# A gather-bound graph network layer: sets of groups, destinations broadcast by DMA, and one tile of 25 built from on-chip columns

## What is computed

```python
h = maximum(layernorm(x), 0)                       # 12500 x 128
m = relu(concat([h[src], h[dst], ea]) @ w1 + b1) @ w2 + b2     # one row per edge
agg = segment_sum(m, dst)                          # 12500 x 128
gi, gh = agg @ w_ih + b_ih, h @ w_hh + b_hh        # GRU gates
r, z = sigmoid(i_r + h_r), sigmoid(i_z + h_z)
n = tanh(i_n + r * h_n)
out = x + (1 - z) * n + z * h
```

## Time and profile before

| what | value |
|---|---|
| median of 3 runs | 4001.74 us (4001.74 to 4002.7) |
| the profiled execution: own time | 4009.54 us |
| its span, first to last instruction | 4007.8 us |
| mean granted TensorE clock | 0.87 |
| first and last gather begin | 76.1 us and 3988.8 us into the span |
| busy share PE, PE weight load, DVE, ACT, POOL | 75%, 67%, 43%, 32%, 75% |
| DMA | 288 MB, mean 72 GB/s |

### The profile page before, as it was taken

The page is one execution under the profiler, slowest core; times in us unless marked ns, Lnnn a source line. Parts: engine busy times, 40 slices in busy tenths (PEclk is TensorE's granted clock), DMA queues, the critical chain, the costliest instruction groups (busy, mean ns, idle before and its releaser), DMA issues.

```text
span 4007.8 us, 76313 instructions
## 1 busy us (share of the span) xinstructions
PE 2996.9 (75%) x20157; PEld 2691.1 (67%) x20157; DVE 1716.2 (43%) x6014; ACT 1281.7 (32%) x3575; POOL 2991.4 (75%) x3163
## 2 busy tenths in 40 slices
PE   5777777777777777777777777777777777777777
PEld 4667666667666666666666667666666666766666
DVE  6444444444444444444444444444444444444443
ACT  5333333333333323333333333333333333333332
POOL 4777777777777777777777777777777777777776
PEclk8888889888888888888888888888888888888887
DMA  6222222222222222222222222222222222222222
GB/s 187 68 69 69 69 69 69 69 69 70 69 69 69 70 70 69 69 69 70 69 69 69 69 69 70 69 69 69 70 69 69 69 69 69 69 69 69 69 69 56
DMA packets 275619, 287.99 MB, mean 72 GB/s; under 512 B 153847, under 2 KB 204696, under 8 KB 275475
## 3 DMA queue, kind: packets, MB, share of 16 engines
q0 software_dynamic: 100000, 205.00, 20.4%
q1 hardware_dynamic: 147282, 69.63, 6.1%
q10 hardware_dynamic: 28318, 13.14, 1.2%
HBM read 274.60 MB, written 12.83 MB: 72 GB/s over the span
## 4 chain that ended last, share of the span: by engine, by line
POOL 71%; issue 26%; DMA 1%; POOLq 1%; DVE 1%; PE 1%; ACT 0%; SPq 0%; DVEq 0%; ACTq 0%
POOL rows L423 71%; POOLq L227 1%; DMA p_rows<-low 1%; POOLq L238 0%; DMA acc<-in_x_dram 0%; DVE stats L700 0%; PE ps L1032 0%; PE ps L1005 0%; DVE mv L706 0%; DVE dst_int L779 0%; DMA onehot<-base_f_dram 0%; DVE low L725 0%; PE ps L1093 0%; PE ps L1094 0%; ACT low L505 0%
## 5 line engine op out<-in xcount | busy, mean ns | idle before, releaser
L423 POOL DMA_INDIRECT rows<-p_rows,idx x3125 | 2960.9, 947 | 964.4 <-issue 952.3
L574 ACT ACTIVATE lhs<-ps 96x640 f32<-96x640 f32 x625 | 437.6, 700 | 2590.5 <-PE ps L1008 2585.4
L1032 PE MATMUL ps<-onehot,rows 128*128 128x95 f32 x6250 | 915.1, 298 | 427.0 <-ACT rows L580 425.9
L1032 PEld LDWEIGHTS ps<-onehot,rows 128*128 128x128 f32 x6250 | 830.6, 210 | 520.9 <-ACT rows L580 290.4
L800 DVE TENSOR_TENSOR rows<-rows,ps 128x640 f32<-128x640 f32 x625 | 512.7, 820 | 1341.3 <-DMA rows<-p_rows,idx 1335.2
L1019 PE MATMUL ps<-rhs,lhs 128*128 128x128 f32 x6250 | 983.8, 315 | 68.9 <-DVE rows L800 68.4
L1019 PEld LDWEIGHTS ps<-rhs,lhs 128*128 128x128 f32 x6250 | 919.0, 229 | 97.2 <-issue 89.9
L1005 PE MATMUL ps<-ident,onehot 128*96 128x128 f32 x3125 | 547.6, 315 | 475.0 <-DVE onehot L790 473.8
L1005 PEld LDWEIGHTS ps<-ident,onehot 128*96 128x96 f32 x3125 | 385.6, 145 | 567.7 <-DVE onehot L790 560.2
L790 DVE TENSOR_SCALAR onehot<-iota_w,dst_int 128x95 f32<-128x95 f32 x3125 | 736.1, 298 | 51.1 <-issue 51.0
L580 ACT ACTIVATE rows<-rows 128x640 f32<-128x640 f32 x625 | 460.0, 736 | 84.6 <-DVE rows L800 82.1
(11 more groups left out here) (94 smaller groups left out, 1307.9 us busy)
## 6 DMA issues: line engine op xcount, KB each, us to landing
rows<-p_rows,idx POOLq DMA_INDIRECT x3125
lhs<-in_ea_t_dram SPq DMA_DIRECT2D x625, 80.0 KB
idx<-in_src_cols_dram SPq DMA_DIRECT2D x625, 2.5 KB
p_rows<-low SPq DMA_DIRECT2D x14, 448.0 KB, 3.6
x_fin<-in_x_dram ACTq DMA_DIRECT2D x123, 50.0 KB
out_dram<-out_fin ACTq DMA_DIRECT2D x123, 50.0 KB
acc<-in_x_dram SPq DMA_DIRECT2D x13, 448.0 KB, 4.8
low<-in_dst_rows_dram SPq DMA_DIRECT2D x1, 1562.5 KB
```

What stands on the lines that cost most here:

```text
L423: pool.indirect_dma_start(out=rows[:, s, t, :], out_offset=None, in_=p_rows[:, :], in_offset=bass.IndirectOffsetOnAxis(ap=idx[:, s, t:t + ...
L574: nc.scalar.activation(lhs[0:WB, s, :], onehotT_ps, ACT.Copy, accum_out=count[:, s:s + 1])
L1032: nc.tensor.matmul(sg[:, 0:W], rows[:, s, t, :], onehot[:, s, t, 0:W], start=(t == 0), stop=(t == T - 1))
```

## The change

**Sets.** The five groups of a chunk form two sets, (0, 1, 2) and (3, 4) (`SETS`). A set has one window, one base, one product with `w1`'s destination part, and its sums stay in PSUM until its last group; `add_segments` runs twice a chunk, and not five times.

**Broadcast destinations.** SP loads each group's 640 destinations to 96 partitions at once (`dst_row`), and DVE compares them with the node number of each partition (`build_lhs`), which gives the transposed one-hot and the count with no transpose and no copy by ACT. `build_onehot` becomes one instruction for five tiles, against 0 to 94 kept in PSUM (`iota_ps`), into one of three places; the destinations relative to the base are made once a chunk (`relative`). The one load of all destination columns and the one subtraction over them (L779) in the setup are gone.

**Stages.** `step(c, s)` on each engine: the SP loads run 3 groups ahead (`AHEAD`), the sums of a group come one step later than before, and the gate steps sit at other places of the chunk.

**One tile without a gather.** Tile 4 of group 3 (`PICKED`) is not gathered. Its 128 source nodes are loaded to registers, and `pick_columns` copies one column of `hT` for each edge into `picked`: in each of steps 0 to 3, 24 columns by ACT and 8 by DVE. PE multiplies `picked` with `w1_keep` (the source part of `w1`) and adds it in PSUM to the tile's `pre_ps`; ACT applies the ReLU from there.

**The end.** `fast()` on each engine is written anew: PE runs `back` of the last gate step, and waits for the last group's `summed` and `onehot_ready`, before the last 200 nodes' products with `h` and before the last `segment_sums`.

The diff, cut to its core:

```diff
-DST_PARTS = LOADS_AHEAD + 1
-IOTA_PARTS = 5
+SETS = ((0, 1, 2), (3, 4))
+ONEHOT_PLACE = (0, 1, 2, 0, 1)
+AHEAD = 3
+PGAP = P + 4
+PICKED = 3
+PICKS_DVE = (8, 8, 8, 8, 0)
+PICKS_ACT = (24, 24, 24, 24, 0)
+def gather_tiles(s):
+    return T - 1 if s == PICKED else T
...
+            def load_destinations(c):
+                wait(sp, dst_rel_ready, c)
+                sp.dma_start(dst_int[:], dst_cols[:, bass.ds(c * (G * T), G * T)]).then_inc(dst_in, 16)
             def load_group(c, s):
-                if not (isinstance(c, int) and c == 0):
-                    load_indices(c, s)
+                wait(sp, lhs_ready[s], c)
+                sp.dma_start(dst_row[:, s, :], dst_rows[bass.ds(c, 1), s * GE:(s + 1) * GE].to_broadcast([WB, GE])).then_inc(dst_row_in[s], 16)
                 wait(sp, pre_ready[s], c)
-                sp.dma_start(lhs[WB:P, s, :], ea_t[:, bass.ds(c * (G * GE) + s * GE, GE)]).then_inc(ea_in[s], 16)
+                sp.dma_start(lhs[WB:P, s, :, 0:P],
+                             ea_t[:, bass.ds(c * (G * GE) + s * GE, GE)].rearrange("f (t p) -> f t p", t=T)).then_inc(ea_in[s], 16)
...
-                    for t in range(T):
+                    for t in range(gather_tiles(s)):
                         pool.indirect_dma_start(
...
+            def load_picks(c, s):
+                if isinstance(c, int) and c == 0:
+                    act.wait_ge(pick_in, 32)
+                _, nodes = nc.values_load_multi_w_load_instructions(
+                    pick_act[0:1, bass.ds(c * N_ACT + sum(PICKS_ACT[:s]), PICKS_ACT[s])], (mybir.EngineType.Activation,),
+                    min_val=0, max_val=N - 1, skip_runtime_bounds_check_because=IN_RANGE)
+                return nodes
+            def pick_columns(c, s, nodes):
+                wait(act, pre_ready[PICKED], c)
+                for e, node in enumerate(nodes, N_DVE + sum(PICKS_ACT[:s])):
+                    last = nc.scalar.copy(picked[:, e:e + 1], hT[:, bass.ds(node, 1)])
+                last.then_inc(picked_act, 1)
...
-            dr = dst_rel.rearrange("p (g t) -> p g t", t=T)
-            nc.vector.tensor_tensor(dr, dst_int[:, :].rearrange("p (g t) -> p g t", t=T),
-                                    base_bc.unsqueeze(2).to_broadcast([P, GROUPS, T]), ALU.subtract).then_inc(dst_rel_ready, 1)
...
+            def relative(c):
+                dve.wait_ge(dst_in, c * 16 + 16)
+                wait(dve, onehot_ready[G - 1], c)
+                for k, members in enumerate(SETS):
+                    tiles = slice(members[0] * T, (members[-1] + 1) * T)
+                    last = nc.vector.tensor_scalar(dst_rel[:, tiles], dst_int[:, tiles], base_bc[:, bass.ds(c * NSETS + k, 1)], None,
+                                                   ALU.subtract)
+                last.then_inc(dst_rel_ready, 1)
             def build_onehot(c, s):
-                wait(dve, seg_ready[s], c)
-                for t in range(T):
-                    last = nc.vector.tensor_scalar(onehot[:, s, t, 0:W].rearrange("p (b a) -> p b a", b=W // IOTA_PARTS),
-                                                   iota_w[:, :, 0:W // IOTA_PARTS],
-                                                   dst_rel[:, bass.ds(c * (G * T) + s * T + t, 1)], None, ALU.is_equal)
-                last.then_inc(onehot_ready[s], 1)
+                user = onehot_holder(c, s)
+                if user:
+                    dve.wait_ge(seg_ready[user[1]], user[0] + 1)
+                dve.wait_ge(dst_rel_ready, c + 1)
+                nc.vector.tensor_tensor(onehot[:, ONEHOT_PLACE[s], :, 0:W],
+                                        dst_rel[:, s * T:(s + 1) * T].unsqueeze(2).to_broadcast([P, T, W]),
+                                        iota_ps.unsqueeze(1).to_broadcast([P, T, W]), ALU.is_equal).then_inc(onehot_ready[s], 1)
+            def build_lhs(c, s):
+                dve.wait_ge(dst_row_in[s], c * 16 + 16)
+                wait(dve, pre_ready[s], c)
+                wait(dve, counted[SET_OF[s]], c)
+                nc.vector.tensor_scalar(lhs[0:W, s, :, 0:P], dst_row[0:W, s, :].rearrange("w (t p) -> w t p", t=T),
+                                        node_at[0:W, bass.ds(c * NSETS + SET_OF[s], 1)], 0.0, ALU.is_equal, ALU.add,
+                                        accum_out=count[0:W, s:s + 1]).then_inc(lhs_ready[s], 1)
...
             def segment_sums(c, s):
...
+                first, last = s in STARTS, s in ENDS
                 for t in range(T):
-                    nc.tensor.matmul(sg[:, 0:W], rows[:, s, t, :], onehot[:, s, t, 0:W], start=(t == 0), stop=(t == T - 1))
+                    done = nc.tensor.matmul(sg[:, 0:W], rows[:, s, t, :], onehot[:, ONEHOT_PLACE[s], t, 0:W], start=(first and t == 0), stop=(last and t == T - 1))
...
             def fast():
                 segment_sums(c, G - 2)
-
-                pe.wait_ge(lhs_ready[G - 1], CHUNKS)
+                back(CHUNKS - LAG - 1)
+
+                pe.wait_ge(rhs_ready[NSETS - 1], CHUNKS)
                 pe.wait_ge(summed[G - 2], CHUNKS)
+                pe.wait_ge(summed[G - 1], CHUNKS)
+                pe.wait_ge(onehot_ready[G - 1], CHUNKS)
```

More of the change, by code:

```diff
@@ L45 @@
 BMAX = N - W
-IOTA_PARTS = 5
-assert W % IOTA_PARTS == 0
 FN = N // CHUNKS
@@ L53 @@
 LN = LAG * FN
+SETS = ((0, 1, 2), (3, 4))
+NSETS = len(SETS)
+SET_OF = {s: k for k, members in enumerate(SETS) for s in members}
+STARTS = {members[0]: k for k, members in enumerate(SETS)}
+ENDS = {members[-1]: k for k, members in enumerate(SETS)}
+ONEHOT_PLACE = (0, 1, 2, 0, 1)
[4 more added lines that the diff above has]
+PICKS_ACT = (24, 24, 24, 24, 0)
+N_DVE, N_ACT = sum(PICKS_DVE), sum(PICKS_ACT)
+assert N_DVE + N_ACT == P
+IN_RANGE = "src holds node indices, 0 to N - 1"
+BASE_IN_RANGE = "the window's base is a least node index, and a minimum holds it at BMAX"
 D = 128
@@ L232, in before, with after, exists, onehot_holder @@
             return None if isinstance(c, int) and c2 < 0 else (c2, s2)
+        def after(c, s, ahead):
+            return (c, s + ahead) if s + ahead < G else (c + 1, s + ahead - G)
+        def exists(group):
+            return group is not None and not (isinstance(group[0], int) and group[0] >= CHUNKS)
+        def onehot_holder(c, s):
+            return before(c, s, next(b for b in range(1, G + 1) if ONEHOT_PLACE[(s - b) % G] == ONEHOT_PLACE[s]))
+        def set_before(c, k):
+            c2, k2 = (c, k - 1) if k else (c - 1, NSETS - 1)
+            return None if isinstance(c, int) and c2 < 0 else (c2, k2)
         def over_chunks(eng, body, first=0):
@@ new lines, in fast @@
+            def fast():
+                load_destinations(0)
+                for s in range(AHEAD):
+                    load_group(0, s)
+                sp.wait_ge(acc_zeroed, 2)
+                for par in range(2):
+                    sp.wait_ge(p_stored[par], BATCHES // 2 * 16)
+                    sp.wait_ge(hT_kept[par], BATCHES // 2)
+                sp.dma_start(deg[0:1, 0:N], acc[0:1, 0:N]).then_inc(deg_zeroed, 16)
+                sp.wait_ge(ranges_ready, 1)
+                sp.wait_ge(w2ih_copied, 2)
+                tile = PICKED * T + T - 1
+                nodes = src_tiles.rearrange("(c k) p -> k c p", k=G * T)[tile:tile + 1, :, :]
+                for row, first, last in ((pick_dve, 0, N_DVE), (pick_act, N_DVE, P)):
+                    sp.dma_start(row.rearrange("o (c e) -> o c e", e=last - first), nodes[:, :, first:last]).then_inc(pick_in, 16)
+                over_chunks(sp, chunk)
@@ new lines, in sum_counts, with load_picks @@
+            def sum_counts(c, k):
+                members = SETS[k]
+                for s in members:
+                    dve.wait_ge(lhs_ready[s], c + 1)
+                wait(dve, seg_ready[members[-1]], c)
+                nc.vector.tensor_reduce(set_count[0:W, k:k + 1], count[0:W, members[0]:members[-1] + 1], AX.X, ALU.add).then_inc(counted[k], 1)
+            def load_picks(c, s):
+                if isinstance(c, int) and c == 0:
+                    dve.wait_ge(pick_in, 32)
+                _, nodes = nc.values_load_multi_w_load_instructions(
+                    pick_dve[0:1, bass.ds(c * N_DVE + sum(PICKS_DVE[:s]), PICKS_DVE[s])], (mybir.EngineType.DVE,),
+                    min_val=0, max_val=N - 1, skip_runtime_bounds_check_because=IN_RANGE)
+                return nodes
@@ L795, in add_pre, with pick_columns @@
+            def pick_columns(c, s, nodes):
+                wait(dve, pre_ready[PICKED], c)
+                for e, node in enumerate(nodes, sum(PICKS_DVE[:s])):
+                    last = nc.vector.tensor_copy(picked[:, e:e + 1], hT[:, bass.ds(node, 1)])
+                last.then_inc(picked_dve, 1)
             def add_pre(c, s):
+                k = gather_tiles(s)
                 dve.wait_ge(pre_ready[s], c + 1)
-                dve.wait_ge(rows_in[s], c * (16 * T) + 16 * T)
-                r = rows[:, s, :, :].rearrange("p t f -> p (t f)")
@@ L1123, in general @@
```

(2 more changed lines are left out.)

348 lines of the change are left out of this document (201 added, 147 removed).

## The result

The changed kernel takes 3857.26 us (median of 4, 3851.49 to 3858.77), the kernel before on the same chip 4001.74 us (4000.62 to 4002.7). The ratio is 0.9636, with a 95% interval of 0.9624 to 0.9648: 144.5 us less. The forecast was 3851 us. The profiled execution took 3857.86 us, its span is 3856.0 us.

The account below looks back on a forecast made before the run. GpSimd's gathers, one per 1.25 us, were taken as the bound. Terms -156.4 - 2.8 + 0 + 3 + 5 = -151.2 us from 4001.7 gave 3851 us; range 3840 to 4015, own case 3840 to 3889.

Parts of the forecast that it names:

- Gathers: GpSimd's loop: 125 fewer gathers at 1.2515 us each, -156.4 us if GpSimd stays the bound.
- The subtraction L779: Setup on DVE: removing the big two-input subtraction, which held one gather, saves 2.8 us.
- The start: First steps: first gather's wait unchanged, buffers needed back only after 24 gathers; 0 us (-2 to +8).
- ScalarE, 17.8 us a turn: ACT's work per chunk with ReLUs, 96 copies and four register loads: 17.8 of 30.04 us, so it fits.
- The first rival: ACT's register loads pay 0.287 us a number and become the bound: some 5100 to 5600 us; 17 in 100.
- VectorE, 20.5: DVE's work per chunk with the new compares, copies and register loads: 20.5 of 30.04 us, so it fits.
- TensorE, lighter: PE loses 25 transposes and three window products, gains one tile, and gets lighter than 23.7 us a chunk.
- Collisions, +3: Loop: DVE's new operations, chiefly the one-column copies, holding gathers; 3 us taken, between 0 and 31.
- The second rival: GpSimd's port held by `build_lhs` or the copies: up to 168 us, 4019 us; 20 in 100.
- DMA traffic, 0: Loop: broadcast loads raise traffic from 69 to about 112 GB/s without slowing the gathers; 0 us.
- The end, +5: After the last gather: last sums begin 5 us later, behind `back` and the products with `h`; +2 to +7.
- The lower bound: Fastest time of the forecast's own case: 3840 us, with nothing for collisions, +2 at the end, -2 at the start.

Follow-up runs that it names:

- four kernels without a hole: Kernels in which GpSimd has no stall at the start, as when nothing is copied or the pick lists are loaded ahead of the flag.
- the control: The changed kernel run again unaltered, beside the kernel before (4002.4 us): 3853.4 us.
- e1_all_gathered: Changed kernel with all 25 tiles gathered and no column copied; 155.0 us more than with 24 gathered and no copies.
- e2_copies_unused: Changed kernel with all 25 tiles gathered and all 128 copies a turn made but never read; quiet interval 1248.3 ns, stall at the start 6.2 us.
- e3_no_copies: Changed kernel with 24 tiles gathered, no lists and no copies, the 25th tile's source part left out; 155.0 us less than with all gathered.
- the second group: Four variants of the changed kernel on a slower chip, where the kernel before takes 5472.0 us; they took 4974.4 to 5628.8 us.
- the kernel without the gap: Changed kernel without the four-column gap between the tiles of `lhs`, on the slower chip: 4974.4 us, ratio 0.9094 to the kernel before.
- the third group: Follow-up kernels on a chip where the kernel before takes 4002.4 us and the changed kernel 3853.4 us.
- the same doubling in three steps: Changed kernel with ScalarE's register loads and column copies done twice in steps 0 to 2 of every turn: 4385.6 us, on the slower chip 5628.8.

## Why the prediction was right, and where its terms were not

The mechanism held: GpSimd sets the time, 125 gathers fewer are the gain, and the other engines' new work fits beside the 24 that are left. By its steps:

- **Gathers, -156.4.** Measured -156.0 (125 x 1.2483; 155.0 between two kernels that differ in little else).
- **The subtraction L779, -2.8.** In the four kernels without a hole all intervals above 1.265 us together cost 0.2 to 0.9 us. Right.
- **The start, 0 (-2 to +8).** This was the step that failed: +13.5 us in the profiled execution, outside its bounds, and 7.5 in the control. I weighed when the buffers would be needed back, and not when the first copies could begin: SyncE issues the lists behind the flag, three groups and `deg`, and ScalarE's first ReLU is queued behind its copies. Loading them early removes it.
- **ScalarE, 17.8 us a turn.** Measured 30.0 - 9.7 = 20.3. Two errors partly cancel: a load of 24 numbers takes 1.66 us, not 0.3, and a copy 0.093 us, not 0.13 (24 in 2.3 us). So 4 x (1.66 + 2.3) = 15.9 us in place of 13.7. The first rival had its mechanism half right, each number is paid, but at 0.05 to 0.06 us, under half the 0.13 at which ScalarE would have become the bound. By the Trainium skill's 200 ns a register ("Runtime: NRT & Kernel Launch", Instruction fetch mechanics) the estimate was 4600 us; the measurement decides against that figure for a load from SBUF.
- **VectorE, 20.5.** Busy 269.4 / 500 x 30 = 16.2 us, and 4 x 0.62 in loads: 18.6. `build_lhs` with its accumulator read took 0.95 us (1.01), the one-hot 0.64 (0.65).
- **TensorE, lighter.** It ran fewer products, 2128 in 500 us against 2540, but was busy 393.8 / 500 x 30 = 23.6 us a turn, as before: the granted clock fell from 0.87 to 0.72. It stayed off the path in the loop.
- **Collisions, +3.** Nothing: e1_all_gathered, e2_copies_unused and e3_no_copies have the same quiet interval and the same 944 ns. The second rival is excluded for these operations, and its price for a kind that does collide was some three times too high (0.17 against 0.054 us).
- **DMA traffic, 0.** Right: 112 GB/s and a share of 0.45 with an unchanged rhythm.
- **The end, +5.** The delay of the sums was +4.75; 1.9 came back by TensorE's clock in that execution, so +2.9. In the control the clock gave nothing, and it was 24.0 - 19.0 = +5.0.

The sum of the measured terms: -156.0 - 2.8 + 13.5 + 2.9 = -142.4, against -144.5 between the medians. With the control's start and end, 7.5 and 5.0, it is -146.3 against 3853.4 - 4002.4 = -149.0. Between the profiled executions it is 4009.54 - 3857.86 = 151.7. The missing 9 us are not the change's: the profiled execution of before has gathers of 947 ns and quiet intervals of 1250.7 ns, where all kernels on the quiet chips have 944 to 945 and 1248.2 to 1249.3, also the one with all 25 gathers, and 2.4 ns x 3124 = 7.5 us is nearly the 7.8 us by which that execution lies over its median. I took the rhythm of one execution and subtracted the 7.8 at the end; that the two belong together is argued, since no second trace of before exists. For the profiled pair the forecast was 3858.3 us, and 3857.86 came: that closeness is chance, the start's +13.5 against the 7.5 of the rhythm, the 3 of the collisions and the 2.1 of the end. The lower bound was also added wrongly: its own terms give 3842.5, not 3840. The range took the result for the right reason only because the start's term was small against 156.

## What to carry to other kernels

Where one engine's instruction count sets the time, work that moves to engines with room is free in the steady loop, and what is left to pay sits at the two ends: follow the first turn's inputs from their issue on, past everything ahead of them in the same queue, because a prologue that is late by some us stalls the bound engine once the buffers are full. Cost a multi-register load per number, and count a loop body's instructions on each engine before making it longer: here 281 brought no pause and 379 cost 2.5 us a turn, more than the work that no longer fitted. Take a rhythm from more than one execution before working with differences of 0.2%.

## What the hardware showed that I had not expected

- On ScalarE a register load of 24 numbers takes 1.66 us, one of 1 number 0.29 us in the kernel before and 0.46 in the changed one: 52 to 60 ns for each further number. On VectorE 8 numbers take 0.62 us.
- ScalarE's one-column copies follow each other every 93 ns, each with its register operation of 37 ns, though each takes 187 ns from start to end.
- The pause after the branch back on ScalarE: 0.20 us in a body of 232 or 281 instructions, 2.83 us (2.46 on the other chip) in one of 379.
- The chip of the second group: before takes 5472 us in place of 4002, and the four kernels on it show SyncE's, ScalarE's and VectorE's register instructions stretched. Two lines of SyncE's queue at the loop's end, the kernel without the gap there and the changed kernel in the third group:

```profile
L285 SPq FUSED_REGOPS  x120: 17/304/718, 234.0 to 4868.5; - x120
```
```profile
L285 SPq FUSED_REGOPS  x120: 41/41/51, 195.2 to 3761.1; - x120
```

  The gathers themselves are as short as elsewhere (945 ns); GpSimd waits some 3 us at a time for sums and for semaphores. That the changed kernel has none of this on another chip, and that the same doubling in three steps takes 4385.6 us there and 5628.8 here, shows that it belongs to the chip; what causes it stays open. Even there the change gains, by 9% with this or that small edit, though the changed kernel itself was not run on it.
